# Second matrix product of an adaptive-LoRA FFN layer as seven quarter products

## What is computed

```python
w   = cond_weight[id[b]]                     # one of 8 matrices 1024 x 1024
y   = x[b] @ w.T                             # first product
base = y @ W_up.T                            # second product, 1024 x 1024, same for all batches
logits = y @ gate_w.T + expert_bias          # 4 experts
z   = y @ lora_A.T                           # rank 8 for each of 4 experts: 32 columns
out[b] = x[b] + base + (z masked to the expert with the largest logit) @ lora_B
```

## Time and profile before

| | |
|---|---|
| Median of 3 runs | 399.13 us |
| Span of the profiled execution | 397.9 us |
| PE busy | 379.4 us, 95% |
| DVE (VectorE) busy | 213.9 us, 54% |
| ACT (ScalarE) busy | 145.4 us, 37% |
| POOL (GpSimd) busy | 17.5 us, 4% |
| DMA moved | 63.65 MB, mean 160 GB/s |

### The profile page before, as it was taken

One profiled execution on the slowest core, in us unless ns is written; L12 is line 12 of the kernel. 1 busy time (PEld: TensorE's weight loads), 2 busy tenths in 40 slices (PEclk: granted clock), 3 DMA queues, 4 the chain that ended last, 5 costly groups with the idle time before them and its releaser, 6 DMA issues.

```text
span 397.9 us, 6753 instructions
## 1 busy us (share of the span) xinstructions
PE 379.4 (95%) x2240; PEld 355.0 (89%) x2240; DVE 213.9 (54%) x484; ACT 145.4 (37%) x316; POOL 17.5 (4%) x17
## 2 busy tenths in 40 slices
PE   2899869999999999999999999999999999999996
PEld 2689759889998999889998899988999899988996
DVE  3768495645546347456366455473573553654132
ACT  4766620637015340356105470153503452053100
POOL 0007520000000000000000000000000000000000
PEclk9999988999999999999999999999999999999999
DMA  6897856652096322971257611864229712450002
GB/s 187 300 360 224 261 216 190 239 203 82 24 285 202 146 105 84 273 230 45 105 137 283 213 50 55 248 225 160 105 60 267 234 71 105 146 170 0 0 0 105
DMA packets 21365, 63.65 MB, mean 160 GB/s; under 512 B 2544, under 2 KB 3696, under 8 KB 21360
## 3 DMA queue, kind: packets, MB, share of 16 engines
q1 hardware_dynamic: 21072, 63.07, 47.8%
q10 hardware_dynamic: 288, 0.52, 0.4%
HBM read 55.20 MB, written 8.39 MB: 160 GB/s over the span
## 4 chain that ended last, share of the span: by engine, by line
PE 87%; DMA 4%; DVE 4%; ACT 2%; SPq 1%; issue 1%; POOL 1%; ACTq 0%
PE ps_o L461 31%; PE ps_y L450 28%; PE ps_y L452 14%; PE ps_o L470 13%; PE ps_o L485 2%; DMA w_raw<-w_dram 2%; DMA lb_raw<-lora_b_dram 2%; DVE w_lo L346 2%; DVE x_hilo L339 1%; ACT up_hi L280 1%; POOL up_lo L244 1%; PE ps_y L478 0%; SPq L133 0%; SPq L149 0%; SPq L197 0%
## 5 line engine op out<-in xcount | busy, mean ns | idle before, releaser
L450 PE MATMUL ps_y<-x_hilo,w_hi 128*128 128x512 f32 x512 | 180.3, 397 | 9.4 <-DVE w_lo L346 7.8
L452 PE MATMUL ps_y<-x_hilo,w_lo 128*128 128x256 f32 x512 | 142.7, 279 | 0.0
L450 PEld LDWEIGHTS ps_y<-x_hilo,w_hi 128*128 128x128 f32 x512 | 96.8, 189 | 32.7 <-issue 7.4
L452 PEld LDWEIGHTS ps_y<-x_hilo,w_lo 128*128 128x128 f32 x512 | 97.0, 189 | 0.0
L346 DVE TENSOR_TENSOR w_lo<-w_raw,w_hi 128x512 fp32r<-128x512 f32 x128 | 81.4, 686 | 3.5 <-ACT w_hi L276 1.3
L461 PE MATMUL ps_o<-up_hi,y_hi 128*128 128x366 f32 x256 | 75.9, 337 | 1.9 <-POOL up_lo L244 1.9
L461 PE MATMUL ps_o<-up_lo,y_hi 128*128 128x366 f32 x256 | 74.8, 333 | 0.0
L461 PE MATMUL ps_o<-up_hi,y_lo 128*128 128x366 f32 x256 | 74.8, 333 | 0.0
L276 ACT CAST w_hi<-w_raw 128x512 fp32r<-128x512 f32 x128 | 71.3, 621 | 2.3 <-DMA w_raw<-w_dram 2.1
L296 ACT COPY y_small<-ps_y 128x256 f32<-128x256 f32 x64 | 23.8, 372 | 121.4 <-PE ps_y L452 121.4
L396 DVE TENSOR_TENSOR y_full<-ps_y,y_small 128x256 f32<-128x256 f32 x64 | 27.1, 424 | 68.8 <-ACT y_small L296 68.8
(11 more groups left out here) (33 smaller groups left out, 177.8 us busy)
## 6 DMA issues: line engine op xcount, KB each, us to landing
w_raw<-w_dram SPq DMA_DIRECT2D x63, 512.0 KB, 4.1
rows<-x_dram SPq DMA_DIRECT2D x16, 512.0 KB, 5.3
x_raw<-xT_dram SPq DMA_DIRECT2D x30, 256.0 KB, 7.0
up_raw<-w_up_dram SPq DMA_DIRECT2D x8, 512.0 KB, 6.7
out_dram<-rows SPq DMA_DIRECT2D x8, 512.0 KB, 7.7
out_dram<-rows SPq DMA_DIRECT2D x8, 329.0 KB, 7.2
out_dram<-rows SPq DMA_DIRECT2D x8, 183.0 KB, 6.7
x_raw<-xT_dram ACTq DMA_DIRECT2D x2, 256.0 KB, 3.4
```

The lines of the kernel that those rows point to most:

```text
L450: pe.matmul(ps_y[c % 2][:, :], w_hi[:, c % RING, cols], x_hilo[:, k, :], start=(k == 0), stop=False)
L452: last = pe.matmul(ps_y[c % 2][:, S:2 * S], w_lo[:, c % RING, cols], x_hilo[:, k, 0:S], start=False, stop=(k == KC - 1))
```

## The change

The second product is cut into quarters: `W_up` into `B11, B12, B21, B22` (512 by 512) and `y` of a batch into `A11, A12, A21, A22` (128 tokens by 512 features). Strassen's algorithm in Winograd's form gives the four output quarters from seven quarter products. It needs four sums of `W_up`'s quarters (T1 to T4, made once, in batch 0, by GpSimd, 16 instructions of 512 columns), four sums of `y`'s (S1 to S4, five VectorE instructions a batch), and seven sums that are made by accumulating in PSUM or by `add_row`. A product is 12 matmuls of 512 columns. The residual, added by eight `add_row` instructions of 512 columns, now partly lies between the products, since a bank is read between two products that accumulate in it.

The gate and LoRA-A columns are computed apart (`gates`: 16 matmuls of 256 columns, transposed; `logits`: 4 small ones that fold high and low parts and transpose back). `choose` runs once a batch for both halves.

Splits are made in place: the raw load lies where the low part will be (`w_raw` is `w_lo`, `x_raw` the low half of `x_hilo`). So a slot of `w` can be loaded only when PE has used it (`w_used`), and `x` only when the first product is over. The ring has 8 slots of half a tile. `x_lo` of batches 1 to 7 moves from VectorE to GpSimd. In batch 0, `W_up`'s splits are 28 of 512 columns on ScalarE, 20 on VectorE and 8 on GpSimd.

```diff
+    FIRST_HALF = (B11, T3, T2, B21, T1)
+    UP_AFTER = {3: 0, 5: 1, 6: 2, 7: 3}
+    UP_ON_DVE = [(q, k) for c in sorted(UP_AFTER) for k in (UP_AFTER[c],) for q in FIRST_HALF]
+    UP_ON_POOL = [(q, k) for q in (T4, B22) for k in range(Q)]
...
             def load_w(b, c, i):
+                    sp.wait_ge(w_used, b * UNITS + g - RING + 1)
...
             def load_x(b, q):
+                    sp.wait_ge(w_used, b * UNITS)
...
             def store_rows(b, t):
+                sp.wait_ge(row_step, b * ROW_STEPS + 6 + 2 * t)
+                sp.dma_start(out[b, t * P:(t + 1) * P, :], rows[:, t, :]).then_inc(stored[t], 16)
...
+            for g in range(2, RING):
+                load_w(0, g, i)
+            load_up(0)
+            for g in range(RING, RING + 6):
+                load_w(0, g, i)
+            load_up(1)
+            for g in range(RING + 6, UNITS):
+                load_w(0, g, i)
+            load_up(2)
+            load_up(3)
...
+            with sp.Fori(1, B - 1) as b:
+                i = adapter(b)
+                for t in range(T):
+                    store_rows(b - 1, t)
+                for g in range(RING, UNITS):
+                    load_w(b, g, i)
+                for t in range(T):
+                    load_rows(b, t)
+                i = adapter(b + 1)
+                for g in range(RING):
+                    load_w(b + 1, g, i)
+                for q in range(XQ):
+                    load_x(b + 1, q)
...
         @block.gpsimd
+            for k in range(Q):
+                pool.wait_ge(up_top_in[k], 16)
+                pool.wait_ge(up_low_in[k], 16)
+                add(up_raw[:, T3, k, :], up_raw[:, B22, k, :], up_raw[:, T1, k, :], ALU.subtract).then_inc(up_sum, 1)
...
+                add(up_raw[:, T4, k, :], up_raw[:, B21, k, :], up_raw[:, T2, k, :], ALU.subtract).then_inc(up_sum, 1)
...
+            with pool.Fori(1, B) as b:
+                for q in range(XQ):
+                    pool.wait_ge(x_hi_ready, b * XQ + q + 1)
+                    ks = slice(q * XK, (q + 1) * XK)
+                    add(x_hilo[:, ks, S:2 * S], x_raw[:, ks, S:2 * S], x_hilo[:, ks, 0:S].bitcast(F32), ALU.subtract
+                        ).then_inc(x_ready, 1)
...
         @block.scalar
+            def first_product(b, first=False):
                 for c in range(OC):
+                    small(b, c)
+                    if c < OC // 2:
+                        for g in range(RING + 2 * c, RING + 2 * c + 2):
+                            w_hi_part(b, g)
...
+            def second_product(b, first=False, last=False):
...
+                    for q, k in UP_ON_POOL:
+                        up_hi_part(q, k)
+                    act.wait_ge(lb_in, 4 * 16)
+                    act.copy(lb_parts[:, :], lb_raw[:, :]).then_inc(lb_hi_ready, 1)
...
+                if not last:
+                    for g in range(4):
+                        w_hi_part(b + 1, g)
...
+                act.wait_ge(g_done, b + 1)
...
         @block.vector
+            def up_lo_part(n, q, k):
+                dve.wait_ge(up_hi_ready, n + 1)
+                if q != T1:
+                    dve.wait_ge(up_sum, 4 * k + 4)
...
+            def first_product(b, first=False):
                 for c in range(OC):
...
+                    full(b, c)
+                    if c < OC // 2:
+                        for g in range(RING + 2 * c, RING + 2 * c + 2):
+                            w_lo_part(b, g)
...
+                    if first and c in UP_AFTER:
+                        for q in FIRST_HALF:
+                            up_lo_part(n_up, q, UP_AFTER[c])
...
+            def second_product(b, first=False, last=False):
...
+                dve.wait_ge(product_done, b * PRODUCTS + 2)
+                add_row(b, 2, 1, 1, ps_v)
+                y_lo_part(b, 7, S4)
+                next_w(0, 1)
+                dve.wait_ge(product_done, b * PRODUCTS + 3)
+                add_row(b, 3, 1, 0, ps_u)
+                next_w(2, 3)
+                dve.wait_ge(g_small_ready, b + 1)
...
+                choose(b)
+                next_w(4, 5, 6, 7)
+                dve.wait_ge(lora_done, b * 4 + 1)
+                add_row(b, 5, 0, 1, ps_u)
...
         @block.tensor
+            def second_product(b):
+                pe.wait_ge(y_ready, b * PRODUCTS + 1)
+                product(b, ps_u, A11, B11, True, False)
+                pe.wait_ge(y_ready, b * PRODUCTS + 2)
+                product(b, ps_v, S3, T3, True, False)
...
+                product(b, ps_p2, A12, B21, True, False)
+                pe.wait_ge(y_ready, b * PRODUCTS + 6)
+                gates(b)
+                pe.wait_ge(row_step, b * ROW_STEPS + 3)
+                product(b, ps_u, S1, T1, False, False)
+                logits(b)
+                product(b, ps_v, A22, T4, False, False)
...
+                product(b, ps_u, S4, B22, False, False)
+                pe.wait_ge(z_parts_ready, b + 1)
+                for t in range(T):
+                    transpose_z(b, t)
...
+                pe.wait_ge(zt_ready, b * T + 1)
+                add_lora(0, 1, ps_u, False)
+                add_lora(0, 0, ps_p2, False)
```

More of the change, by code:

```diff
@@ L55, in sem @@
         def sem(name):
             return ctx.enter_context(nc.semaphore(name))
[L58 to L66, removed]
+        w_raw, w_lo = sb_raw("w_lo", [P, RING, HK * P])
@@ L67, in build @@
+        w_hi = sb("w_hi", [P, RING, HK * P], F32R)
+        x_raw, x_hilo = sb_raw("x_hilo", [P, KC, 2 * S])
+        up_raw, up_lo = sb_raw("up_lo", [P, PRODUCTS, Q, HALF])
+        up_hi = sb("up_hi", [P, PRODUCTS, Q, HALF], F32R)
+        y_raw, y_parts = sb_raw("y_parts", [P, PRODUCTS, Q, 2, P])
         y_small = sb("y_small", [P, 2, S])
[L68 to L70 removed]
         rows = sb("rows", [P, T, H])
+        gl_raw = sb("gl_raw", [P, 3 * Q, GL])
@@ L453, in first_product @@
                                          start=False, stop=(k == KC - 1))
-                    last.then_inc(y_done, 1)
-            def bank_ab(t, c, banks=(0, 1)):
-                toks = slice(t * P, (t + 1) * P)
-                for n, (y, up) in enumerate(((y_hi, up_hi), (y_hi, up_lo), (y_lo, up_hi))):
-                    for k in banks:
-                        pe.matmul(ps_o[t][:, k, 0:CUT], y[:, c, toks], up[:, c, k * CUT:(k + 1) * CUT],
-                                  start=(c == 0 and n == 0), stop=False)
@@ L464, in bank_c @@
-            def bank_c(t, c):
-                toks = slice(t * P, (t + 1) * P)
-                terms = [(y_hi, up_hi, NW), (y_hi, up_lo, H), (y_lo, up_hi, H + GL)]
-                for y, up, end in terms if c < OC - 1 else terms[::-1]:
-                    last = pe.matmul(ps_o[t][:, 2, 0:end - 2 * CUT], y[:, c, toks], up[:, c, 2 * CUT:end],
-                                     start=(c == 0 and end == NW), stop=(c == OC - 1 and end == NW))
-                if c == OC - 1:
-                    last.then_inc(z_done, 1)
+                        if k % HK == HK - 1:
+                            last.then_inc(w_used, 1)
@@ new lines, in product @@
+            def product(b, ps, p, q, start, stop):
+                terms = [(k, y, up) for k in range(Q) for y, up in ((0, up_hi), (0, up_lo), (1, up_hi))]
+                for n, (k, y, up) in enumerate(terms):
+                    if isinstance(b, int) and n % 3 == 0:
+                        if (q, k) in UP_ON_DVE:
+                            pe.wait_ge(up_ready[0], UP_ON_DVE.index((q, k)) + 1)
+                        else:
+                            pe.wait_ge(up_ready[1], UP_ON_POOL.index((q, k)) + 1)
+                    last = pe.matmul(ps[:, :], y_parts[:, p, k, y, :], up[:, q, k, :], start=start and n == 0,
+                                     stop=stop and n == len(terms) - 1, skip_group_check=True)
+                last.then_inc(product_done, 1)
@@ new lines, in gates @@
+            def gates(b):
+                if isinstance(b, int):
+                    pe.wait_ge(gl_ready, 1)
+                n = 0
+                for t, p, m in ((0, A11, 0), (0, A12, 1), (1, S1, 0), (1, A22, 2)):
+                    for k in range(Q):
+                        last = pe.matmul(ps_g[0:2 * GL, t * 2 * P:(t + 1) * 2 * P], gl_parts[:, m * Q + k, :],
+                                         y_parts[:, p, k, :, :].rearrange("p j n -> p (j n)"),
+                                         start=(n == 0), stop=False, skip_group_check=True)
+                        n += 1
+                last.then_inc(g_done, 1)
@@ new lines, in logits @@
+            def logits(b):
+                if isinstance(b, int):
+                    pe.wait_ge(eye_ready, 2)
+                pe.wait_ge(g_ready, b + 1)
+                for t in range(T):
+                    for part in (g_hi, g_lo):
+                        last = pe.matmul(ps_z[:, t * GL:(t + 1) * GL], part[0:2 * GL, t, :], fold[0:2 * GL, :],
+                                         start=(t == 0 and part is g_hi), stop=False, skip_group_check=True)
```

(1 more changed line is left out.)

548 lines of the change are left out of this document (304 added, 244 removed).

## The result

The changed kernel takes 422.18 us (median of 4 runs, 421.23 to 423.77), the kernel before 398.91 us beside it: ratio 1.0596, 95% interval 1.0554 to 1.0639. It is 23 us slower; 417 us was forecast, range 402 to 432.

What follows compares the result with a forecast made beforehand. PE's issue rate was taken to bound the kernel before, and the port shared by VectorE and GpSimd the changed batch 0: 87.5 + 7 x 46.0 + 5.9 = 415.4 us of span, plus 1.2 us, 417 us; range 402 to 432.

Steps and rivals of the forecast that it cites:

- PE's sum: In a steady batch's second product: PE's work sums to 22.95 us against 24.50 us before, 1.55 us less.
- The fourth rival: In PE's quarter products: 512-column matmuls take 0.24 us instead of 0.228, 8 us more, 425 us; chance 3%.
- The port in batch 0: In batch 0: VectorE's and GpSimd's two-SBUF-input instructions pass one at a time; product 2 starts at 59 us, batch 1 at 87.5.
- The first rival: In batch 0: GpSimd's sums overlap freely with VectorE's work; batch 0 takes 69 us, the kernel 392 us; chance 6%.
- The start of the count: In batch 0: the first 4 MB of loads landed at 18.3 us, and 40.5 us more pass until product 2.
- x_lo on GpSimd: In a steady second product: four `x_lo` cost VectorE 5.2 us between 8 and 15 us, with no loss but no slack.
- the signs named: In the profile after: second products 22.9 us, gap before tile 3, product 2 near 59 us, batch 1 near 87, POOL some 75 us busy.
- the 59% range: For the whole kernel: batch 0 83 to 91 us, batches 45.5 to 46.8 us, so 409 to 424 us; chance 59%.
- The ring: In steady first products: slots of `w` reload only after PE's use, units 8 and 9 behind stores; 0 to 2 us a batch.
- The chain of tile 1: In a steady first product: tile 1's copies queue behind unit 9's splits, so tile 3 starts at 8.9 us instead of 8.33.
- The term of 0.85 us a batch: In each steady batch: the wait for the ring of `w`, taken as 0.85 us from a range of 0 to 2 us.
- The end: After PE's end: the last four additions run after the last LoRA matmul, then a 512 KB store; 5.9 us against 3.6.

Runs made afterwards that it cites:

- the kernel with late splits: The changed kernel with the splits of units 8 to 15 one tile later on ScalarE and VectorE, DMA order unchanged: 410.58 us, ratio 1.029.

## Why the prediction was right, step by step

**PE's sum held.** Twelve matmuls of 512 columns took 2.72 to 2.84 us (0.228 each, forecast, is 2.74), the gates 1.87 us (1.9), the logits 0.37 us (0.4), transposes to LoRA-B 0.58 us (0.6), four LoRA-B matmuls 1.03 us (0.9). Sum 23.1 against 22.95 us. The fourth rival, dearer quarter products, did not come. The Trainium skill ("TensorE: Matmul & The Clock Gate", "Wait — 56ns, not 53.3ns?") gives columns at 2.4 GHz and about 2.5 ns, 0.216 us for 512 columns; the trace does not agree, with 0.227 us at the least.

**The port in batch 0 held.** Product 2 started at 56.5 us (forecast 59), batch 1 at 84.3 us (87.5), and the run without the sums shows their part in it, 11.3 us. The first rival (free overlap, 69 us) is out by 15 us. The start of the count was a little late: the first load of `W_up` had landed at 16.46 us, where 18.3 was taken. From there to product 2 it took 40.0 us, and 40.5 was forecast, but the parts are not those of the forecast. The 16 sums were taken at their full 20.6 us. VectorE's instructions were stretched by 14.7 us in all, because a sum cost it 1.07 us and not 1.29, and because not every sum met one of them. The rest is what the forecast had put at nothing: VectorE was idle for 3.5 us of the 40 and spent 2.9 us on seven `full`.

From product 2 to batch 1 27.8 us passed (forecast 28.5). That agreement is luck in good part. The logits came 17.8 us after product 2's start, where 22 us were forecast, since the queues ahead of them were shorter than laid out. From the logits to batch 1 10.0 us passed, where 7 were forecast. The forecast of batch 0 has no term for TensorE's clock and none for `choose` beside GpSimd. The rows are a window (columns as in the earlier trace rows) of product 2, a step of `choose` and a wait of PE:

```profile
56.45:61.74 5.29, 5.29 (x13) 4.13 (x13) 5.17 (x7) 4.50 (x10) 1.91 (x2) 0.50 0.00 0
...
76.78 2.07 DVE L462 TENSOR_TENSOR pick<-score,smax 128x8 f32<-128x8 f32 x1
...
PE ps_y L627 <- DVE z_parts L473: 1.4, 1, 1.4
```

Product 2 ran at half clock from start to end, after three waits of 1.7 to 2.8 us, and took 5.3 us instead of 2.7. The LoRA-B matmuls, after the wait for `z_parts`, took 0.43 us each instead of 0.23. A step of `choose` with 8 columns took 2.07 us while GpSimd ran LoRA-B's low part of 1024 columns; the median of the eight batches is 0.17 us. The run without the sums has the same 27.9 us for this stretch.

**x_lo on GpSimd cost nothing in a steady batch**, as laid out; two runs show it, one on either kernel.

**Of the signs named** one missed: GpSimd was busy for 94.0 us, not some 75, because its instructions of 512 columns took 1.62 to 1.72 us on the mean, not 1.29. And the upper end of the 59% range does not follow from its terms: 91 + 7 x 46.8 + 7.1 is 426 us, not 424. The result lies inside either way.

**The ring held in its place, and was undersized.** The chain of tile 1 is as forecast, in batch 4 (starts at 227.42 us):

```profile
234.04 1.32 ACT L318 CAST w_hi<-w_lo_raw 128x512 fp32r<-128x512 f32 x2 [3.23 <-DMA w_lo_raw<-w_dram]
235.26 0.37 ACT L329 COPY y_small<-ps_y 128x256 f32<-128x256 f32 x1
...
236.54 0.50 PE L585 MATMUL ps_y<-x_hilo,w_hi 128*128 128x512 f32 x1 [0.49 <-DVE y_parts_raw L426]
```

`small(1)` at 7.8 us into the batch, tile 3 at 9.1 us, where I had 8.9. But the sentence that later units never wait is wrong: `full` of a later tile is held in the same way (gaps of up to 0.3 us ahead of tile 6 in batches 4 to 7), and PE's pairs of matmuls ran up to 6 ns apart more in such batches (see below). The term of 0.85 us a batch measured 1.2 us.

**Batch 1 was mis-sized.** I took it for a steady batch. It took 50.5 us: 2.25 us of gap ahead of tile 3, since the row additions of batch 0 ended at 88.7 us, 4.4 us into the batch instead of 2.1, and unit 8's load was issued at 89.97 us; and PE ran at 1.2 GHz at its start, after the waits of batch 0, and again after the gap (granted clock 0.90 over the window of 27.39 us). In batches 2 to 7, with gaps of at most 0.76 us, the granted clock was 1.00. I had `next_w` in VectorE's list of batch 0, but not what it does to the stores that the next batch's loads stand behind. This term alone is 4.5 us; with 0.5 us too little in each of six batches, 3.2 us too much in batch 0 and 0.6 us too much at the end it makes the 3.5 us between the spans (415.4 and 418.9).

**The end** took 5.3 us (5.9): each of the last two stores landed 2.7 us after its issue, where 3.7 us (2.76 and 0.9) were taken.

## What to carry to other kernels

Work given to GpSimd beside a busy VectorE isn't free help when both read two operands from SBUF: each sum on GpSimd spared VectorE 0.6 us and, where the two met, cost it 1.07 us. A ring that frees its slots later must be paid for in the order of the engines behind it: the copy that frees PE's bank belongs ahead of the split that waits for a load. And a sum that gains per iteration has to be set against its preparation in the first one: 8 iterations of 1.9 us barely paid for it.

## What the runs showed of the hardware that was not expected

The pairs of 512 and 256 columns in the first product run at one of two spacings with no wait between them: 0.347 us in batches 1 to 7 of the kernel before, and 0.347 or 0.353 us on the mean in the changed one, alike through a tile or a whole batch and changing mostly at a gap (in batch 1 it went from 0.353 to 0.347 us between tiles 5 and 6 with none). In the kernel with late splits this is all that differs between its first products of 22.19 and 22.61 us. What sets it is open.

GpSimd's two-input instruction of 512 columns took 1.26 us at the least and 1.62 to 1.72 us on the mean beside VectorE's. And the loads of 256 KB in batch 4's first product landed in 2.9 to 3.5 us, hardly sooner than one of 512 KB in the kernel before (3.3 us); the first load of the group behind them took 2.5 to 2.6 us in batches 2 to 6. Halving the tile did not halve the wait.
